# Key rope tables built inside the key loop, and bf16 LayerNorm sums, in a transformer layer on 8 cores

## What is computed

```python
q_c  = _rms_norm(x @ wq_down.T, q_norm_w)            # q_nope, q_pe from q_c
kv_c = _rms_norm(x @ wkv_down.T, kv_norm_w)          # k_nope, v from kv_c
k_rope_shared = (x @ wk_rope.T)
cos, sin = _rope_cos_sin(seq_len, 64)
q_pe = _apply_rope(q_pe, cos, sin)
k_rope_shared = _apply_rope(k_rope_shared, cos, sin)
out = softmax(causal(q @ k.T * scale)) @ v ;  attn = out @ wo.T
x = _layernorm(x + attn)
x = _layernorm(x + shared_mlp(x) + routed_mlp(x) * comb_w)
# _layernorm: m = mean(x); v = var(x); (x - m) / sqrt(v + 1e-5)
```

## Time and profile before

| | us |
|---|---|
| two runs | 4131.62 and 4257.84, median 4194.73 |
| profiled execution, whole | 4135.05 |
| its span, slowest core (core 7) | 4133.9 |
| spans of the other cores | 4061.7 to 4132.6 |
| stage B, from the first load to the barrier | about 434 to 818 |
| first LayerNorm | about 2188 to 2322 |
| second LayerNorm | about 3988 to 4112 |

### The profile page before, as it was taken

How to read it: one execution, slowest core, us unless ns; L and a number is a source line. 1 busy time by engine, 2 the same in 40 slices (tenths; PEclk the granted TensorE clock), 3 DMA queues, 4 the chain that set the end, 5 groups by cost and what they waited for, 6 DMA issues and landing times.

```text
span 4133.9 us, 39769 instructions; the slowest of 8 cores (4061.7 to 4133.9 us)
## 1 busy us (share of the span) xinstructions
PE 3162.0 (76%) x14466; PEld 1357.0 (33%) x14466; DVE 1453.9 (35%) x2079; ACT 847.5 (21%) x1011; POOL 311.2 (8%) x377
## 2 busy tenths in 40 slices
PE   2667147578777777878496489999999989999983
PEld 0223012234243333323241034444444434444430
DVE  2112544455555555464313322122221212222144
ACT  0111012154545454454201000000000000000011
POOL 1001100000000000000010011101101110111100
PEclk9989569878678767766698789999999999999996
DMA  9044514333534444353680454956649484674702
GB/s 131 1 56 65 70 21 65 47 68 60 102 58 78 85 75 84 61 93 60 164 88 3 62 50 49 96 72 62 81 42 102 63 81 62 61 90 50 86 1 81
DMA packets 716975, 281.59 MB, mean 68 GB/s; under 512 B 662257, under 2 KB 695537, under 8 KB 716658
## 3 DMA queue, kind: packets, MB, share of 16 engines
q0 software_dynamic: 405776, 181.69, 37.6%
q1 hardware_dynamic: 311010, 97.35, 11.7%
HBM read 348.99 MB, written 18.87 MB: 89 GB/s over the span
## 4 chain that ended last, share of the span: by engine, by line
PE 63%; DVE 14%; DMA 11%; issue 5%; ACT 3%; SPq 1%; another core or an unknown queue 1%; DVEq 0%; POOL 0%; ACTq 0%; POOLq 0%
PE pdnE L1309 12%; PE puE L1274 11%; PE pgE L1266 10%; DMA Pt<-P 4%; PE pOC L905 4%; DMA wuE<-su 3%; DVE smx L863 3%; PE pdD L1072 3%; PE paC L770 3%; PE paC L832 3%; PE paC L836 3%; PE pkvB L560 3%; PE paC L743 3%; PE pqcA L329 2%; SPq L891 1%
## 5 line engine op out<-in xcount | busy, mean ns | idle before, releaser
L1266 PE MATMUL pgE<-x1b,wgE 128*128 128x512 bf16 x2304 | 529.5, 384 | 25.2 <-DMA wgE<-sg 23.1
L1274 PE MATMUL puE<-x1b,wuE 128*128 128x512 bf16 x2304 | 530.5, 384 | 18.2 <-DMA wuE<-su 18.2
L1309 PE MATMUL pdnE<-O_sb,wdE 128*128 128x512 bf16 x2304 | 503.6, 382 | 23.9 <-issue 23.9
L832 PE MATMUL paC<-K,qnC 128*128 128x512 bf16 x576 | 292.1, 507 | 189.3 <-ACT S L849 134.1
L1285 DVE CAST usE<-puE 128x512 bf16<-128x512 f32 x144 | 99.6, 692 | 877.8 <-ACT gsE L1281 520.9
L1281 ACT ACTIVATE gsE<-pgE 128x512 bf16<-128x512 f32 x144 | 86.0, 597 | 1425.4 <-PE puE L1274 1221.1
L863 DVE TENSOR_REDUCE smx<-S 128x1 f32<-128x4096 f32 (+7 forms) x128 | 326.8, 2553 | 19.6 <-DVE S L856 6.1
L1266 PEld LDWEIGHTS pgE<-x1b,wgE 128*128 128x128 bf16 x2304 | 227.0, 99 | 305.7 <-issue 40.9
L1274 PEld LDWEIGHTS puE<-x1b,wuE 128*128 128x128 bf16 x2304 | 227.3, 99 | 298.7 <-issue 33.5
L1309 PEld LDWEIGHTS pdnE<-O_sb,wdE 128*128 128x128 bf16 x2304 | 226.0, 98 | 301.5 <-issue 34.6
L796 ACT ACTIVATE P<-S,smn 128x4096 bf16<-128x4096 f32 (+7 forms) x128 | 283.3, 2213 | 163.5 <-DMA Pt<-P 156.3
(11 more groups left out here) (192 smaller groups left out, 2413.4 us busy)
## 6 DMA issues: line engine op xcount, KB each, us to landing
wgE<-sg POOLq DMA_DIRECT2D x64, 512.0 KB, 8.4
wuE<-su POOLq DMA_DIRECT2D x64, 512.0 KB, 10.0
wdE<-sd POOLq DMA_DIRECT2D x64, 512.0 KB, 16.5
xkB<-xf POOLq DMA_DIRECT2D x8, 2048.0 KB, 18.0
xsum<-xo SPq DMA_DIRECT2D x1, 8192.0 KB, 44.2
woD<-wo POOLq DMA_DIRECT2D x16, 512.0 KB, 6.5
out<-xsum SPq DMA_DIRECT2D x1, 8192.0 KB, 22.0
wqd_sb<-wqd POOLq DMA_DIRECT2D x1, 6144.0 KB, 68.0
```

The lines of the kernel that those rows point to most:

```text
L832: ten.matmul(pa[w][:, bk * 512:bk * 512 + 512], qn_sl[u][:, qc0:qc0 + 128], K2[:, hh * S + o: hh * S + o + 512], start=True, stop=False)
L1266: i = ten.matmul(pg[w][:], wg_sl[sl][:, dc * 128:(dc + 1) * 128], x1b[:, dc * TOK + tt * 512: dc * TOK + tt * 512 + 512], start=(dc == 0), ...
L1274: i = ten.matmul(pu[w][:], wu_sl[sl][:, dc * 128:(dc + 1) * 128], x1b[:, dc * TOK + tt * 512: dc * TOK + tt * 512 + 512], start=(dc == 0), ...
L1309: i = ten.matmul(pdn[w][:], wd_sl[dsl][:, oc * 128:(oc + 1) * 128], h_buf[:, ic2 * TOK + tt * 512: ic2 * TOK + tt * 512 + 512], start=(ic2 ...
```

## The change

Stage B: two chunks of the key tables are built ahead of the key loop instead of eight. Chunk kb + 2 is built inside block kb, for kb from 0 to 5: its instructions are issued behind the block's `pkr` matmuls and behind `load_xk(kb + 2)`, and ahead of the block's norm. The rope of a block has a further wait, for its own chunk.

`emit_ln`: ScalarE first copies the block of `xsum` to bf16 (`xbd`, two buffers), and then squares the copy into `sqd`, which is now bf16 too. Both column sums take bf16 operands and a bf16 column of ones. Both calls are changed.

```diff
-            for c_ in range(8):
+            tb_done = {}
+
+            def build_k_tables(c_):
                 build_tables_chunk(kpos(c_),
                                    cosk_all[:, c_ * 512:(c_ + 1) * 512],
-                                   sink_all[:, c_ * 512:(c_ + 1) * 512], scrB)
+                                   sink_all[:, c_ * 512:(c_ + 1) * 512],
+                                   scrB)
+                tb_done[c_] = s_tb.n
+
+            build_k_tables(0)
+            build_k_tables(1)
 
             for kb in range(8):
...
                 s_xkf[sl].inc(i)
                 if kb + 2 < 8:
                     load_xk(kb + 2)
+                    build_k_tables(kb + 2)
                 s_sqB[(NKC - 1) % 2].wait(vec)
...
                 s_tb.wait(vec)
                 s_krdma.wait(vec)
+                vec.wait_ge(s_tb.h, tb_done[kb])
...
             sqd = [stL.enter_context(
-                nc.sbuf_tensor(f"sqD{tag}{i}", [128, 512], F32))
+                nc.sbuf_tensor(f"sqD{tag}{i}", [128, 512], BF16))
+                for i in range(2)]
+            xbd = [stL.enter_context(
+                nc.sbuf_tensor(f"xbD{tag}{i}", [128, 512], BF16))
                 for i in range(2)]
...
                     s_sq[w].wait(sca)
                     s_ln.wait(sca)
-                    s_sq[w].inc(sca.activation(sqd[w][:], xsl, AF.Square))
+                    s_sq[w].inc(sca.activation(xbd[w][:], xsl, AF.Copy))
+                    s_sq[w].wait(sca)
+                    s_sq[w].inc(sca.activation(sqd[w][:], xbd[w][:],
+                                               AF.Square))
...
-                    i = ten.matmul(pstv[:], ones_c[:], sqd[w][:],
+                    i = ten.matmul(pstv[:], ones_cb[:], sqd[w][:],
                                    start=(dc == 0), stop=(dc == NDC - 1))
                     s_sq[w].inc(i)
-                    i = ten.matmul(pstm[:], ones_c[:], xsl,
+                    i = ten.matmul(pstm[:], ones_cb[:], xbd[w][:],
                                    start=(dc == 0), stop=(dc == NDC - 1))
```

## The result

| | before | changed |
|---|---|---|
| profiled execution | 4135.05 us | 4137.52 us |
| its slowest core | 4133.9 us | 4136.3 us |
| lowest run | 4122.71 us | 4137.52 us |
| median of all runs shown | 4184.86 us (38 runs) | 4155.39 us (39 runs) |

The ratio is 1.0025, with a 95% interval of 1.0012 to 1.0037: the changed kernel is slower, by 5 to 15 us, and by less than 2%. The medians of all runs point the other way because many runs of both kernels were disturbed, some by 400 us; the ratio compares undisturbed ones alone.

The account below looks back on a forecast made before the run. TensorE's idle gaps in stage B's serial table chunks and its two-pass float32 matmuls in the norm were taken as the bounds. 4135.05 + 48.2 (stage B) - 32.6 (norm) = 4150.7, so 4151 us, +0.4%, bounds 4139 and 4161.

Parts of the forecast that it names:

- The base: Whole kernel: the profiled execution of 4135.05 us, to which the predicted gains and losses were added.
- The norm, 32.6: LayerNorm statistics: four halves take 87.6 us against 120.2, a gain of 32.6 us, bounds 27.2 and 37.4.
- Removed, 101.6: Front of stage B: six of eight chunks leave, saving 101.6 us, bounds 99.2 and 102.7.
- The chunk, 22.5 each: Blocks 0 to 5 of stage B: the norm's L592 starts 22.5 us later in each, 135.0 us.
- Sqrt, 1.28 in five blocks: Key loop of stage B: an added Sqrt table load of 1.28 us in five blocks, 6.4 us.
- The cold return, 1.4: Six blocks of stage B: TensorE comes back at the low clock, 1.4 us a block, 8.4 us.
- Stage B in all: Stage B: 149.8 us added less 101.6 removed, +48.2 us, from +41.5 to +53.1.
- 1: Rival, stage B: the chunks hide behind matmuls; 4001 us, faster by 3.2%; chance 0.03.
- 2: Rival, stage B: TensorE stays at 1.2 GHz through the six blocks; 4251 us, slower by 2.8%; chance 0.05.
- 3: Rival, norm: waiting for its own Copy costs ScalarE 0.5 us, cadence near 1.7, no gain; 4183 us; chance 0.08.
- 4: Rival, ScalarE: a table switch costs its 1.28 us a second time, 14 us more; 4165 us; chance 0.09.

Follow-up runs that it names:

- Experiment 6: The changed kernel with four buffers instead of two for the norm's bf16 copy and square; VectorE's wait in four norm halves 85.6 us against 94.2.
- experiment 3: The changed kernel with only chunk 0 built ahead and the chunks inside the loop cut up among later instructions; stage B 309.8 us, slowest core 4024.4 us against 4136.3.
- experiment 4: The changed kernel with Copy in place of Sin in the six chunks inside the loop (wrong output); stage B 417.2 us, 14.4 us less.
- ln_only: The kernel before with only the LayerNorm part of the change; ratio to before 0.9924 (0.9899 to 0.9949).
- b_only: The kernel before with only the stage B part of the change, LayerNorm as before; ratio to before 1.0129 (1.0085 to 1.0172).

## What the prediction had right, and the steps that failed

The prediction said +0.4%, made of +48 us and -33 us; measured are +0.25% (0.12 to 0.37), and +45 and -26 by the stages. The forecast mechanism is the one that the experiments showed. Two steps failed: the base on which the time was given, and the size of the norm's pace. In order:

- **The base.** The prediction summed on one execution, 4135.05 us, and gave the result, 4151 us, as its time. That is a slowdown only against this base. Beside the median in the table of times, 4194.73, the same number reads as a gain of 1%, and the runs showed no gain: the changed kernel is 5 to 15 us slower. The prediction saw that its base was 60 us below the median and said it in a side remark ("Against that median the same sum is 4210."), but did not carry it into the forecast. The 38 runs of before span 4122.71 to 4554.21 us, so a change of 16 us can be given as a ratio and not as a time. Even as a ratio, +0.4% lies just above the interval.
- **The norm, 32.6.** This is the term of the sum that was mis-sized most: it measured 26.1. The pace was taken as 1.28 us a column block, and is 1.38. The loop over the same buffer, Copy, Square, pair of matmuls, Copy, was worked out in the text at 1.35 and set aside as "inside the range". It was the longer of the two and so the bound; a loop's pace is the largest of its limits, not a middle. With 1.35 the gain would have been 28, with 1.38 it is 27. Experiment 6 shows that this loop was the bound.
- **Removed, 101.6.** On core 1 the first tile landed 37.4 us after its issue and not 34.9, and the first Copy came 40.0 us after the first ptb (97.2 us sooner than before, I had 99.2); the second group ran in 3.6 as foreseen. In all 99.6, and 100.6 in the mean of 8 cores.
- **The chunk, 22.5 each.** On core 1 it was 20.5 in block 0 and 21.6 to 22.7 in the other five, 130.8 in all, and the mean of the cores is 130.9, where I had 135.0. Two things were mis-sized: at ptb TensorE ran faster than foreseen (1.01 us, not 1.88), and block 0 needs no Sin load, since the chunks ahead of the loop had left the table in place. So there are ten added loads and not 11.
- **Sqrt, 1.28 in five blocks.** From L600 to the reciprocal it takes 2.89 us in blocks 1 to 5, against 1.51, so 1.38; in block 0, where both kernels load, it is 3.05 against 2.78, as the Sqrt also waits for the last Sin (520.97). In all 7.2, where I had 6.4.
- **The cold return, 1.4.** From pbc to Copy it is 8.0 us in the mean of the cores against 6.5, so 1.5 and nearly right. The cores differ: core 1, with the longest stage B, has 8.3, and core 7 of before 6.2, which makes 2.1.
- **Stage B in all.** 130.8 + 7.2 + 12.3 - 99.6 = 50.7 by these figures of core 1 against core 7 of before, whose stage lengths give 50.5 (434.4 against 383.9). These are the longest and the shortest. In the mean it is 130.9 + 7.2 + 9.2 - 100.6, less 2.0 by which the later groups and the end of the stage ran sooner: 44.7, and 44.6 was measured. That the forecast of 48.2 came so near is in part luck: 4.1 too much for the chunks and the 2.0 that it did not have stand against 1.6 too little for Sqrt and the return and 1.0 too much for what was removed. In the whole sum, too, the norm's 6.5 us too much and stage B's 3.6 too much cancel in part: +15.6 forecast, +18.5 by the stages.
- **Rivals.** 1 did not happen, and experiment 3 shows what it needs: the chunk cut up, 33.5 us a block. 2 did not: on core 1 the groups behind the first ran in 3.6 us. 3 is refuted by the handover, 0.09 us from Copy to Square. 4 is refuted by experiment 4.
- **The whole against its parts.** +18.5 by the stages, +10.4 (5 to 15) by the ratio. The two profiled executions show where the 8 us lie, but not why. The mean of the cores' spans is 4097.9 before and 4108.3 changed, also +10.4; beside the 44.7 and -26, stages C and D together are 5.8 us shorter (1362.0 to 1356.2) and stages A and E 2.6. The code there is the same, the cores of one execution differ by 25 us in C and D and by 58 in stage E, and with ln_only, whose stage B is the old one, C and D took 1363.5, with b_only 1360.8. So it may be chance; whether later stages give back a few us stays open. Nor does the longest stage B make the slowest core: core 7 of before was the slowest with the shortest, 383.9, since its stage E was the longest.

## What to carry to other kernels

Moving work into a loop hides it only if nothing that the loop waits for stands behind it in any engine's queue: ask of each piece what follows it on that engine, and cut it up where the answer is the critical chain. A chain across four engines cost nearly its whole length in both places where it stood in front, ahead of the norm and ahead of the next block's Copy; the same 21 operations cost 25 us a block ahead of the norm, and some 4 when cut up and placed behind the instructions that the loop waits for. Before spreading serial small work over a loop, look whether it can be made wide (32 partitions to 128), and let an engine that only waits do the conversion for the one that is busy.

## What the runs showed of the hardware

- A switch of ScalarE's table cost its load of 1.28 us and next to nothing else: 1.32 us each over ten switches where they stand, 1.44 by the stage's length, also where the load began 0.02 to 0.18 us behind a Sin.
- Filling TensorE's wait with matmuls brought the next group back at or near full speed, but the low clock then showed in the group behind it in some blocks; 1.9 us a block won locally, 0.6 kept.
- In the norm's halves the granted clock was 0.93 to 1.00 with float32 passes. With bf16 pairs every 1.38 us in the mean it was 0.57 and 0.50 in the two halves of the first norm, and with pairs every 0.52 us 1.00.
